# One burst of 256-column products per tile in the steady loop of a cross-attention kernel

## The reference, cut to what matters

```python
q = heads(query, Wq, bq, Sq)                                  # 128 rows
k = heads(key, Wk, bk, Sk)                                    # 12544 rows, 512 wide
v = heads(value, Wv, bv, Sk)
q_prime = relu(einsum('bhnd,fd->bhnf', q, Wqf))
k_prime = relu(einsum('bhnd,fd->bhnf', k, Wkf)) * attention_mask[:, None, :, None]
kv = einsum('bhnf,bhne->bhfe', k_prime, v)
k_sum = sum(k_prime, axis=2)
out = einsum('bhmf,bhfe->bhme', q_prime, kv) / (einsum('bhmf,bhf->bhm', q_prime, k_sum) + 1e-08)
x = x + out @ Wo.T + bo
```

## Time and profile before

| | |
|---|---|
| median of 3 runs | 862.82 us (862.41 to 862.89) |
| profiled execution, span from first to last instruction | 860.8 us |
| PE busy | 851.4 us, 4618 matmuls |
| DVE busy | 683.3 us |
| ACT busy | 554.7 us |
| POOL busy | 370.6 us |

### The profile page before, as it was taken

How to read it: one execution, slowest core, us unless ns; L and a number is a source line. 1 busy time by engine, 2 the same in 40 slices (tenths; PEclk the granted TensorE clock), 3 DMA queues, 4 the chain that set the end, 5 groups by cost and what they waited for, 6 DMA issues and landing times.

```text
span 860.8 us, 14422 instructions
## 1 busy us (share of the span) xinstructions
PE 851.4 (99%) x4618; PEld 731.0 (85%) x4618; DVE 683.3 (79%) x1075; ACT 554.7 (64%) x1009; POOL 370.6 (43%) x215
## 2 busy tenths in 40 slices
PE   8999999999999999999999999999999999999998
PEld 7888888888888888888888888888888889878767
DVE  5777777777777777777777777888888878779897
ACT  5666666666666666666666666666777656676563
POOL 2555454544555554445445555544454433220000
DMA  7212214010101010010101010101101000679740
GB/s 271 98 51 76 73 52 167 24 49 24 49 24 49 24 49 25 30 43 24 49 24 49 24 49 24 48 25 28 46 24 49 26 1 11 239 282 410 308 147 13
DMA packets 19529, 66.25 MB, mean 77 GB/s; under 512 B 2224, under 2 KB 2992, under 8 KB 19120
## 3 DMA queue, kind: packets, MB, share of 16 engines
q1 hardware_dynamic: 19072, 64.88, 20.9%
q10 hardware_dynamic: 432, 1.05, 0.3%
HBM read 65.66 MB, written 0.26 MB: 77 GB/s over the span
## 4 chain that ended last, share of the span: by engine, by line
PE 91%; issue 4%; DVE 2%; DMA 1%; POOL 1%; ACT 0%; POOLq 0%; ACTq 0%; SPq 0%; DVEq 0%
PE kv_ps L879 11%; PE f_ps L866 11%; PE v_bank L784 10%; PE v_bank L785 10%; PE v_bank L786 10%; PE k_bank L784 10%; PE k_bank L785 10%; PE k_bank L786 10%; PE kv_ps L1178 2%; PE kv_ps L1160 1%; DMA early<-in_wk 1%; PE f_ps L949 0%; PE f_ps L1050 0%; PE v_bank L968 0%; DMA ctx_raw<-in_ctx 0%
## 5 line engine op out<-in xcount | busy, mean ns | idle before, releaser
L461 POOL TENSOR_TENSOR ksum_acc<-ksum_acc,kf 128x1024 f32<-128x1024 f32 x97 | 233.0, 2402 | 86.7 <-DVE kf L1284 86.7
L454 POOL TENSOR_TENSOR ctx_lo<-ctx_raw,ctx_hi 128x512 fp32r<-128x512 f32 x92 | 119.7, 1301 | 274.0 <-ACT ctx_hi L532 274.0
L540 ACT ACTIVATE keys<-k_bank,bias_cols 64x512 fp32r<-64x512 f32 (+1 forms) x194 | 131.5, 678 | 148.6 <-PE k_bank L786 146.2
L1260 DVE SCALAR_TENSOR_TENSOR keys<-k_bank,bias_cols,keys 64x512 fp32r<-64x512 f32 (+1 forms) x194 | 143.2, 738 | 83.7 <-ACT keys L540 80.4
L1277 DVE TENSOR_TENSOR kf<-f_ps,fb 128x256 f32<-128x256 f32 x392 | 148.6, 420 | 16.8 <-ACT fb L557 5.6
L784 PE MATMUL v_bank<-wv_hi,ctx_lo 128*128 128x512 f32 x388 | 152.3, 392 | 0.0
L785 PE MATMUL v_bank<-wv_lo,ctx_hi 128*128 128x512 f32 x388 | 152.1, 392 | 0.0
L784 PE MATMUL k_bank<-ctx_hi,wk_lo 128*128 128x512 f32 (+1 forms) x392 | 151.4, 386 | 0.0
L785 PE MATMUL k_bank<-ctx_lo,wk_hi 128*128 128x512 f32 (+1 forms) x392 | 151.1, 385 | 0.0
L786 PE MATMUL v_bank<-wv_hi,ctx_hi 128*128 128x512 f32 x388 | 151.0, 389 | 0.0
L786 PE MATMUL k_bank<-ctx_hi,wk_hi 128*128 128x512 f32 (+1 forms) x392 | 149.9, 383 | 0.0
(11 more groups left out here) (245 smaller groups left out, 979.0 us busy)
## 6 DMA issues: line engine op xcount, KB each, us to landing
ctx_raw<-in_ctx SPq DMA_DIRECT2D x46, 512.0 KB, 3.3
early<-in_stream SPq DMA_DIRECT2D x15, 1024.0 KB, 8.4
raw<-in_stream SPq DMA_DIRECT2D x12, 1024.0 KB, 8.7
early<-in_stream SPq DMA_DIRECT2D x8, 512.0 KB, 4.2
early<-in_ctx SPq DMA_DIRECT2D x2, 512.0 KB, 6.1
early<-in_wv SPq DMA_DIRECT2D x1, 1024.0 KB, 7.8
early<-in_wq SPq DMA_DIRECT2D x1, 1024.0 KB, 9.2
early<-in_wo SPq DMA_DIRECT2D x1, 1024.0 KB, 7.1
```

Of the source, the lines that this page charges most:

```text
L454: pool.tensor_tensor(ctx_lo[:, s, :, cols], raw[:, :, t % 2 * P:(t % 2 + 1) * P], ctx_hi[:, s, :, cols].bitcast(f32), ALU.subtract).then_i ...
L461: pool.tensor_tensor(ksum_acc[:, :].rearrange("p (j f) -> p j f", f=P), ksum_acc[:, :].rearrange("p (j f) -> p j f", f=P), kf[:, t % 2, :, ...
L540: act.activation(keys_2[rows, s, 2 * m + h, 0:n], src[rows, 0:n], ACT.Identity, bias=bias_cols[rows, KC + m:KC + m + 1]).then_inc(k_hi_rea ...
L1260: dve.scalar_tensor_tensor(out=keys_2[other, s, 2 * m + h, 0:n], in0=src[rows, 0:n], scalar=bias_cols[rows, KC + m:KC + m + 1], in1=keys_2 ...
```

## The change

In chunks 1 to 23 the order within a tile is now: values of tile `n` (12 matmuls); then jobs 2 and 3 of tile `n`, the key-values of tile `n - 1` and job 0 of tile `n + 1`, together 14 matmuls of 256 columns; then the first matmul of the keys (`key_pass_low`); then job 1 of tile `n + 1`; then the other eleven matmuls of the keys. Jobs 0 and 1 of a tile so run one tile ahead; those of tile 4 are put behind chunk 0, and tile 96 has only jobs 2 and 3 left. ScalarE and VectorE get a `tile_steady` with the same instructions in the new order.

```diff
             def period(c, s, n_keys=CHUNK):
                 n = TILES * c
                 for t in range(TILES):
-                    jobs = [(c, s, n + t, t, i) for i in range(JOBS)]
-                    values(n + t, s, t, jobs[0:2])
-                    keys(c + 1, 1 - s, t, jobs[2:4], n_keys)
+                    pe.wait_ge(v_lo_ready, n + t)
+                    for k in range(KC):
+                        value_step(n + t, s, t, k)
+                    for i in (2, 3):
+                        feature_job(c, s, n + t, t, i)
                     key_values(n + t - 1, t + 1)
+                    first_jobs(c, s, n + t + 1, t + 1, 0)
+                    keys(c + 1, 1 - s, t, (), n_keys, late=lambda i: first_jobs(c, s, n + t + 1, t + 1, i))
...
+                    if late is not None and k == 0:
+                        key_pass_low(s, m, n)
+                        late(1)
+                        last = key_passes_high(s, m, n)
...
+            def first_jobs(c, s, n, t, i):
+
+                if t == TILES:
+                    feature_job(c + 1, 1 - s, n, 0, i)
+                else:
+                    feature_job(c, s, n, t, i)
...
+            def tile_steady(n, t, keys, splits=()):
+
+                for i in (2, 3):
+                    features_share(n, i, False)
+                values_high(n, t, False)
+                for i in (0, 1):
+                    features_share(n + 1, i, False)
+                for x in splits:
+
+                    split_ctx_high(*x)
+                features_high(n, t)
+                keys_high(*keys)
...
+            def tile_steady(n, t, keys):
+
+                for i in (2, 3):
+                    features_sum(n, t, i, False)
+                masked_features(n, t)
+                values_low(n, t)
+                for i in (0, 1):
+                    features_sum(n + 1, t + 1, i, False)
+                features_low(n, t)
+                keys_low(*keys)
...
                 for k in range(KC):
                     value_step(n, s, t, k, k_bank if t else v_bank)
-                    feature_job(*jobs[k])
+                    if t or k >= 2:
+                        feature_job(*jobs[k])
```

More of the change, by code:

```diff
@@ L584, in tile @@
                     keys_high(*k)
+            def tile_steady(n, t, keys, splits=()):
[8 more added lines that the diff above has]
+                keys_high(*keys)
             def tile_before_last(n, t):
-                features_high(n - 1, 1)
-                for i in range(JOBS):
+                for i in (2, 3):
                     features_share(n, i, False)
@@ L611, in period @@
                 for t in range(TILES):
-                    tile(n + t, t, keys=((c + 1, 1 - s, t, k_bank, keys),),
-                         splits=((2 * c + 4 + t // 2, s, t),) if t < splits else ())
+                    tile_steady(n + t, t, (c + 1, 1 - s, t, k_bank, keys),
+                                splits=((2 * c + 4 + t // 2, s, t),) if t < splits else ())
                     if pieces:
@@ L650, in _ @@
                 tile(t, t, first=t < 2, keys=((1, 1, t, k_bank, CHUNK),), splits=((4 + t // 2, 0, t),))
+            for i in (0, 1):
+                features_share(TILES, i, False)
+            features_high(TILES - 1, TILES - 1)
             with act.Fori(1, LAST - 5, 2) as c:
@@ L797, in keys_0, with keys @@
                     last.then_inc(k_done, 1)
-            def keys(c, s, m, jobs, n=CHUNK, apart=False):
+            def keys(c, s, m, jobs, n=CHUNK, apart=False, late=None):
                 pe.wait_ge(ctx_lo_ready, TILES * (c - 1) + n // P)
@@ L804, in keys @@
                 for k in range(KC):
-                    last = three(k_bank[:, 0:n], wk_hi[:, m, k, :], wk_lo[:, m, k, :],
-                                 ctx_hi[:, s, k, 0:n], ctx_lo[:, s, k, 0:n], k == 0, k == KC - 1)
+                    if late is not None and k == 0:
[3 more added lines that the diff above has]
+                    else:
+                        last = three(k_bank[:, 0:n], wk_hi[:, m, k, :], wk_lo[:, m, k, :],
+                                     ctx_hi[:, s, k, 0:n], ctx_lo[:, s, k, 0:n], k == 0, k == KC - 1)
                     if k == KC - 1:
                         last.then_inc(k_done, 1)
+                    if late is not None:
+                        continue
                     if apart:
@@ L814, in keys, with key_pass_low, key_passes_high @@
                             feature_job(*job)
+            def key_pass_low(s, m, n):
+                pe.matmul(k_bank[:, 0:n], wk_lo[:, m, 0, :], ctx_hi[:, s, 0, 0:n], start=True, stop=False)
+            def key_passes_high(s, m, n):
+                pe.matmul(k_bank[:, 0:n], wk_hi[:, m, 0, :], ctx_lo[:, s, 0, 0:n], start=False, stop=False)
+                return pe.matmul(k_bank[:, 0:n], wk_hi[:, m, 0, :], ctx_hi[:, s, 0, 0:n], start=False, stop=False)
             def value_step(n, s, t, k, bank=v_bank):
@@ L905, in period_0 @@
                         key_values(t - 1, t + 1, first=t == 1)
+                for i in (0, 1):
+                    feature_job(1, 1, TILES, 0, i)
+            def first_jobs(c, s, n, t, i):
+                if t == TILES:
+                    feature_job(c + 1, 1 - s, n, 0, i)
+                else:
+                    feature_job(c, s, n, t, i)
             def period(c, s, n_keys=CHUNK):
@@ L1366, in period @@
                         qkv_low(i - 1)
-                    tile(n + t, t, keys=((c + 1, 1 - s, t, k_bank, keys),))
+                    tile_steady(n + t, t, (c + 1, 1 - s, t, k_bank, keys))
             def queries_out():
@@ L1416, in _ @@
                 tile(t, t, first=t < 2, keys=((1, 1, t, k_bank, CHUNK),))
+            for i in (0, 1):
+                features_sum(TILES, 0, i, False)
+            features_low(TILES - 1, TILES - 1)
             with dve.Fori(1, LAST - 7, 2) as c:
```

5 lines of the change are left out of this document (2 added, 3 removed).

## The result

The changed kernel takes **866.97 us** (median of 4 runs, 866.90 to 867.32), the kernel before 862.76 us beside it: ratio 1.0050, interval 1.0036 to 1.0064. It is slower by 4.2 us. The forecast was 862.1, with a range from 860.2 to 864.7. The profiled execution of the changed kernel took 867.32 us, its span is 865.4 us (before: 860.8), and the granted clock is 1.00 in both.

What follows compares the result with a forecast made beforehand. PE was taken as the bound, busy 851.4 of 860.8 us. Terms -2.0 - 0.5 + 1.4 + 0.2 + 0.2 = -0.7 gave 860.1 for the span and 862.1 for the median, range 860.2 to 864.7.

Steps and rivals of the forecast that it cites:

- One burst: PE, 88 tiles of chunks 1 to 22: one width change fewer saves 0.023 a tile, 2.0 us; bounds 0 and 3.5.
- Rival 1: PE's burst stays two bursts because the lone 512-column product starts a width change of its own: 864.1; chance 0.17.
- Job 0 waits for the sum of job 2: PE's weight load in each tile comes 0.015 to 0.02 late; cost taken as 0, bound 0.9 us.
- The first tile of a chunk: ScalarE's stand-alone wait adds 0.08 before job 0: 17 x 0.08 = 1.4 us lost; TensorE's at last tiles 0.2.
- The start: Key-values of tile 3 wait for the features' low part near 58.6: 0.2 us lost, once.
- The end: Tile 96: PE's 0.53 us wait for the features' low part goes; gain 0.5, bounds 0 and 0.5.
- The other waits: VectorE's keys' and features' low parts, pieces of later weights, and banks all stay within slack (1.2 us for keys): no cost.
- three rivals: Burst stays two (864.1, chance 0.17); second change vanishes, chain hides better (860.4, 0.23); job 0 waits in every tile (867.8, 0.13).
- rival 3: Slower: job 0 waits in every tile, 0.08 in the other 71 adding 5.7 us: 867.8; chance 0.13.

Runs made afterwards that it cites:

- experiment 8: Changed kernel with job 1 directly behind job 0, no 512-column key product between them: 877.20 us, ratio 1.0166.
- Experiment 6: ScalarE's two waits in features_share swapped: on the changed kernel 867.00 us; with experiment 4 862.21; with experiment 4, in the loop only, 861.74 (0.9988).
- experiment 4: Changed kernel with all twelve pieces behind the values' low part and, in chunk 23, VectorE's keys' low part ahead of the features' low part: 862.09 us, ratio 0.9990.
- experiment 5: Changed kernel with GpSimd's add ahead of its context split in every tile of the loop: 881.57 us, ratio 1.0215.

## Why the prediction was wrong

- **One burst: right in kind, a little over.** Before, PE had no idle time in either stretch of the earlier trace rows, so its own pace was what could be won there. 0.023 a tile was taken, 0.019 came (7.381 in the mean of the tiles of chunks 1 to 17 that are no chunk's first). Rival 1 (two bursts) would be 7.40. The prediction expected few 512-column starts over 0.23 us behind the lone pair. In the mean of 48 tiles there are three (0.235, 0.234, 0.233) and one ahead of the pair, four in a tile where there were eight before.
- **Job 0 waits for the sum of job 2: right.** It costs nothing where VectorE is free, as 7.38 shows. Its slack is as small as was said: 0.3 us on VectorE's side became 0.33 on TensorE's in the twelve tiles, and experiment 8 took 0.13 out of it.
- **The first tile of a chunk: right.** 0.08 was taken; 7.465 against 7.381 is 0.084, or 17 x 0.084 = 1.4 us. Experiment 6 took it away again.
- **The start: right.** Tile 4 takes 7.60 against 7.40. PE's load for the key-values stands at 58.64 in the changed kernel.
- **The end: the failing step's second half.** Tile 95's low part is indeed ready, but the keys' low part, which nothing had waited for before, came late (PEld idle for 0.9 us above, of which experiment 4 won back 0.8) behind a features' low part of 2.18 us. A gain of 0.5 became a loss of 0.5.
- **The other waits: this step failed.** It said of the stretch with the pieces "not over 1 us in a tile", "still in the slack", "No cost", with the pieces as they were in the trace of before, 0.69 us each, and the features' low part at 1.23. Those durations are of instructions that had GpSimd idle beside them: the piece at 604.08 began 0.01 us before the add's end, and the low part at 57.40 lies between an add that ended at 56.49 and a split that began at 59.64. In the changed kernel, beside GpSimd's instructions, they are 1.22 and 1.47 (2.2 in chunk 23). The step counted work on VectorE but never laid GpSimd's instructions beside it, and it set the slack against the keys' low part alone, while the piece stands between that and the sum of job 2: 1.53 us of keys' low parts end at 614.06, the share is there at 615.02, so 0.96 us were free, enough for 0.69 and not for 1.22. This is 4.0 us (12 tiles of 7.71 against 7.38), and with the end's 0.9 (0.5 lost where 0.4 was to be won, a lone wait's 0.06 counted in) it is nearly all of the distance to the forecast: the sum of the forecast was 860.1 for the span, 865.4 came, of which 4.0 + 0.9 are these two; the rest, 0.4, is mostly the burst at 0.019 and the tenth of tile 76.

The prediction's last sentence named keys' low parts that come late as what would make it wrong; in tile 96 it was that, in the twelve tiles the instruction behind them. None of the three rivals was it: rival 3 had the right place (job 0's wait), the right sign, and a wrong reason, and counted 71 tiles where there were 12.

What the change is worth without its side effect is the kernel of experiment 6: 861.74 us, 0.1% under the kernel before, with the piece, the order at the end and the wait in the loop put right. It is 1.2 us under the kernel before beside it (862.91), by an interval that ends only just under one, at 0.9997, and 5.2 us under the changed kernel.

## What to carry to other kernels

A duration read from a profile belongs to its neighbours, as the piece's 0.69 us did, which became 1.22: before an instruction is moved, look at what GpSimd does at the new time. For the VectorE instructions with two operands in SBUF, "own time plus what is left of GpSimd's, less 0.15 us" was a good estimate in this case: the piece had 0.69 of its own and 0.67 left of the add and took 1.22, the features' low part 1.23 and 0.39 left of the split and took 1.47. The same instruction with two durations in one trace, as the features' low part had in the kernel before (1.23 and 1.45 us), is the sign to look for. Lay every engine that an edit shifts beside the others, even one with 43% busy time: GpSimd was never late itself, and still cost 4 us. And where a chain has lost its slack, ask of every instruction on its engines that stands only in some tiles.

## What was not expected of the hardware

- A VectorE difference of two SBUF operands, 512 columns: 0.69 us alone, 1.22 beside an add of GpSimd that had started; a row sum of the same 512 columns 0.69 in both cases.
- The add of GpSimd, 1024 columns: 2.40 us alone, 3.39 where the features' low part was first; with 128 columns 0.46 alone, and still 1.45 there. In experiment 5 a split of 1.30 us took 1.30 where it started 0.06 us ahead of the low part, and 2.30 where it started behind.
- A ScalarE instruction that the program lets wait for two semaphores carried one of them: none of the 1009 in the changed kernel's trace has two. With constants it was the one written first; with registers it changed from place to place in one order and was the same everywhere in the other. Where the wait that ended last stood apart, a chunk's first tile was 0.08 us longer and a tile outside the loop 0.06.
